# A two-layer graph network on one Trainium2 core: edge units dealt anew, logits made turned, and node sums in 64-node windows

## What is computed

```python
# layer 0, per edge e with source src and destination dst
msg = project_src(node)[src] + project_dst(node)[dst]       # 64 scalars + 32 vectors
m1  = tensor_product(msg, rsh(edge), rbf(edge) @ W_rbf)      # 96 scalars + 128 vectors
a   = leaky(m1_s @ W_alpha).reshape(e, 4, 16)                # leaky: a if a > 0 else 0.2 a
a   = sum(a * alpha_dot, -1)                                 # 4 logits per edge
alpha = softmax of a over the edges of one destination
val = gate(m1_s @ Ws_val, m1_v @ Wv_val); m2 = tensor_product(val, rsh)
agg = segment_sum(alpha * (m2 @ W_vlin), dst)                # then projected, added to x

# layer 1, per edge
w   = silu(rbf @ Wfc1) @ Wfc2
mid = w * tensor_product(f[src], rsh)                        # 384 numbers per edge
n   = segment_mean(mid, dst)                                 # then Wl2, Wa, Wsc per node
```

## Time and profile before

| | us |
|---|---|
| three timed runs | 8655.53, 8661.65, 8667.87 (median 8661.65) |
| profiled execution, span from first to last instruction | 8679.9 |
| PE busy | 7627.6 (88%) |
| DVE busy | 7274.4 (84%) |
| POOL busy | 6016.9 (69%) |
| ACT busy | 3252.4 (37%) |
| mean granted TensorE clock | 0.947 of full |

### The profile page before, as it was taken

How to read it: one execution, slowest core, us unless ns; L and a number is a source line. 1 busy time by engine, 2 the same in 40 slices (tenths; PEclk the granted TensorE clock), 3 DMA queues, 4 the chain that set the end, 5 groups by cost and what they waited for, 6 DMA issues and landing times. The chain is left out here.

```text
span 8679.9 us, 218293 instructions
## 1 busy us (share of the span) xinstructions
PE 7627.6 (88%) x60373; PEld 5771.5 (66%) x60374; DVE 7274.4 (84%) x17597; ACT 3252.4 (37%) x8375; POOL 6016.9 (69%) x5890
## 2 busy tenths in 40 slices
PE   2599999999999999999999999887968888888888
PEld 1487777877877787877787778776644444444445
DVE  4699999999999999999999999775368888888886
ACT  1244444444444444444444444332222222222223
POOL 0477777777777777777777777651037777777774
PEclk9799999999999999999999999987569999999999
DMA  4344444444444444444444444321012222222222
GB/s 53 78 101 99 102 100 101 102 100 101 101 102 101 101 101 99 102 100 100 100 101 102 101 102 100 77 75 29 11 37 67 67 67 67 67 67 67 67 67 61
DMA packets 616622, 725.52 MB, mean 84 GB/s; under 512 B 284132, under 2 KB 390884, under 8 KB 616573
## 3 DMA queue, kind: packets, MB, share of 16 engines
q0 software_dynamic: 225408, 385.00, 20.4%
q1 hardware_dynamic: 391165, 339.92, 15.3%
HBM read 708.40 MB, written 16.06 MB: 83 GB/s over the span
## 5 line engine op out<-in xcount | busy, mean ns | idle before, releaser
L778 PE MATMUL bank_pair<-w_msg,blocks 128*128 128x160 f32 (+2 forms) x15640 | 2078.7, 288 | 126.8 <-DVE blocks L1030 98.2
L720 POOL DMA_INDIRECT got_src<-src_tab,idx x1564 | 1661.5, 1062 | 659.4 <-POOL idx L714 358.5
L778 PEld LDWEIGHTS bank_pair<-w_msg,blocks 128*128 128x128 f32 x15640 | 1972.7, 192 | 218.5 <-DVE blocks L1030 218.5
L1504 POOL DMA_INDIRECT gotf<-f_tab,idx x1568 | 1702.3, 1086 | 514.2 <-issue 477.4
L720 POOL DMA_INDIRECT got_dst<-dst_tab,idx x1564 | 1486.3, 950 | 528.7 <-issue 503.7
L802 PEld LDWEIGHTS bank_pair<-weights_t,product 128*128 128x128 f32 x12896 | 1498.7, 195 | 309.9 <-issue 295.6
L802 PE MATMUL bank_pair<-weights_t,product 128*128 128x128 f32 x12896 | 1575.5, 281 | 9.5 <-ACT weights_t L932 8.2
L1545 PE MATMUL bank_pair<-val,to_node 128*128 128x385 f32 x3136 | 1247.6, 545 | 5.0 <-DVE val L1659 5.0
L1600 ACT ACTIVATE val<-pre,y_edge 128x160 f32<-128x160 f32 x1568 | 542.8, 417 | 1534.0 <-DVE pre L1640 1531.4
L1545 PEld LDWEIGHTS bank_pair<-val,to_node 128*128 128x128 f32 x3136 | 621.6, 208 | 536.8 <-issue 270.1
L767 PE MATMUL bank_pair<-edge,w_edge 64*128 64x512 f32 x3128 | 884.8, 642 | 9.5 <-DVE blocks L1030 9.5
(11 more groups left out here) (268 smaller groups left out, 11950.3 us busy)
## 6 DMA issues: line engine op xcount, KB each, us to landing
rbf<-in_rbf SPq DMA_DIRECT2D x391, 256.0 KB
dst_bc<-in_dst_rows SPq DMA_DIRECT2D x391, 256.0 KB
y<-in_y SPq DMA_DIRECT2D x391, 128.0 KB
y<-in_y SPq DMA_DIRECT2D x391, 96.0 KB
gotf<-f_tab,idx POOLq DMA_INDIRECT x1568, 2.7
got_src<-src_tab,idx POOLq DMA_INDIRECT x1564
got_dst<-dst_tab,idx POOLq DMA_INDIRECT x1564
rbf<-in_rbf SPq DMA_DIRECT2D x392, 32.0 KB, 1.7
```

The lines of the kernel that those rows point to most:

```text
L720: pool.indirect_dma_start(out=buf[slot][:, t, :], out_offset=None, in_=table[:, :], in_offset=bass.IndirectOffsetOnAxis(ap=idx[slot][:, c: ...
L778: return nc.tensor.matmul(to, blocks[rows, k, P * t:P * t + P], w_msg[rows, c0:c1], start=start, stop=stop)
L1504: pool.indirect_dma_start(out=got[k][:, t, :], out_offset=None, in_=f_tab[:, :], in_offset=bass.IndirectOffsetOnAxis(ap=idx[k][:, t:t + 1] ...
```

## The change

In layer 0 the sixteen pieces of the tensor product (32 channels by harmonic) are dealt anew over the four blocks, so that the scalars, the logit inputs and the vectors each need fewer columns: per tile four matmuls of 128, 128, 96 and 64 columns in place of five. The 64 logit inputs are no longer made beside the scalars but turned: `add_alpha` keeps `w_msg` in the array (64 columns) and streams the blocks (256 edges each into one half of the partitions). ACT makes `rl` from that, DVE one operation `leaky` (128 x 256), and `spread_logits` is a matmul with a constant `spread` that holds `alpha_dot`, each entry repeated 32 times; the multiplication, the reduction and `logits_wide` go. Both turned halves of `msg` now lie in different PSUM pairs. In ACT's list the weights come ahead of `th`, and `rl` last but for the copies of the turned message. SP loads 96 instead of 112 rows of `y8` per group.

```diff
-                def message_scalars(t):
-                    add_piece(scalar_tile(t), 0, slice(0, P), t, 0, True, False)
-                    return add_piece(scalar_tile(t), 2, slice(0, P), t, 3, False, True)
...
+                def add_alpha(k, piece, start, stop):
+                    first = MSG_FIRST[piece] + 128
+                    for half in range(2):
+                        last = nc.tensor.matmul(alpha[64 * half:64 * half + 64, :], w_msg[:, first:first + 64],
+                                                blocks[:, k, 256 * half:256 * half + 256], start=start, stop=stop)
+                    return last
+
+                def message_tile(t):
+                    add_piece(t, 0, LOW_S, MSG_C2, MSG_S + 96, True, False)
+                    add_piece(t, 3, HIGH_S, MSG_C2, MSG_S + 96, False, True)
+                    add_piece(t, 2, HIGH_V, MSG_C0, MSG_C1 + 32, True, False)
+                    return add_piece(t, 1, LOW_V, MSG_V, MSG_C1 + 32, False, True)
 
                 def spread_logits(slot):
-                    for t in range(TILES):
-                        last = nc.tensor.transpose(turn_low[:, P * t:P * t + P], logits_wide[slot][:, t, :], ident[:])
+                    for half in range(2):
+                        rows = slice(64 * half, 64 * half + 64)
+                        last = nc.tensor.matmul(spread_out[:, half, :], spread[rows, :], leaky[slot][rows, :], start=True, stop=True)
                     return last
...
                         for t in range(TILES):
-                            last = message_scalars(t)
-                        last.then_inc(s["message_s"], 1)
-                        for t in range(3):
-                            message_vectors(t)
+                            last = message_tile(t)
+                        last.then_inc(s["message"], 1)
+                        if mid:
+                            wait_apart(pe, s["top"], g, s["tick_p"])
+                        add_alpha(0, LOW_S, True, False)
+                        add_alpha(3, HIGH_S, False, True).then_inc(s["alpha"], 1)
                     if mid:
                         pe.wait_ge(s["weights"], g)
                         turn_weights().then_inc(s["weights_turned"], 1)
-                    if now:
-                        message_vectors(3).then_inc(s["message"], 1)
...
+                        if mid:
+                            act.wait_ge(s["leaky"], g)
+                        act.wait_ge(s["alpha"], g + 1)
+                        nc.scalar.activation(rl[:], alpha, ACT.Relu, scale=0.8).then_inc(s["relu"], 1)
...
-                        dve.tensor_tensor(lg[:], lg[:], adot[:].unsqueeze(1).broadcast_to([P, TILES, 64]), ALU.mult).then_inc(s["logit_step"], 1)
...
+                        dve.wait_ge(s["relu"], g + 1)
+                        dve.scalar_tensor_tensor(leaky[slot][:], alpha, 0.2, rl[:], ALU.mult, ALU.add).then_inc(s["leaky"], 1)
```

```diff
+                def add_tile(half, nodes, k, t, start, stop):
+                    for side in range(2):
+                        last = nc.tensor.matmul(win[half][WIN * side:WIN * side + WIN, :], nodes,
+                                                val[k][:, t, HALF1 * side:HALF1 * side + HALF1], start=start, stop=stop)
+                    return last
...
-                    dve.tensor_tensor(to_node[k % 2][:], iota_row[:].unsqueeze(1).broadcast_to([P, TILES, P]),
-                                      slot0[:, tile_dst(g, 1)].unsqueeze(2).broadcast_to([P, TILES, P]), ALU.is_equal)
+                    dve.tensor_tensor(to_node[k % 2][:], iota_row[:, 0:WIN].unsqueeze(1).broadcast_to([P, TILES, WIN]),
+                                      slot0[:, tile_dst(g, 1)].unsqueeze(2).broadcast_to([P, TILES, WIN]), ALU.is_equal)
...
-                    for j, n in enumerate(rows_of):
-                        last = nc.tensor.matmul(pQ[t % 2], turned[t % 2][0:n, j, :], w_last[0:n, j, :], start=j == 0, stop=j == 2)
+                    for k in range(4):
+                        cols = slice(WIN * (k // 2), WIN * (k // 2) + WIN)
+                        for part in range(2):
+                            last = nc.tensor.matmul(pQ[t % 2][WIN * part:WIN * part + WIN, :], turned[t % 2][:, 2 * part + k % 2, cols],
+                                                    w_last[:, k, :], start=k == 0, stop=k == 3)
```

330 lines of the change are left out of this document (176 added, 154 removed).

## The result

The changed kernel takes 8777.45 us (median of 4 runs, 8774.91 to 8791.91), the kernel before 8660.49 on the same chip (8655.53 to 8667.87). The ratio is 1.0135 by the medians, 1.014 with a 95% interval of 1.0125 to 1.0154 as measured: slower by about 117 us. The forecast was 8725 in a range of 8600 to 8850. The direction holds and so does the main mechanism; the size is 52 us short, and several steps behind it were wrong, as the experiments show. Some executions of any of these kernels run several per cent longer, whatever the kernel; medians and ratios here are those of the others.

A forecast was written before the change was run, and what follows sets the result against it. POOL was taken to bound both layers, with holding-up by DVE. Terms +36 - 15 (layer 0), +10 + 12 (layer 1), +22 (last stage) made +65 us: span 8679.9 to 8745, median 18 lower, about 8725; range 8600 to 8850.

The forecast's parts named there:

- POOL sets layer 0: Layer 0: POOL's list of 13.60 us per group plus its gathers' holding-up, 0.56, sets the time.
- the floor of PE that I set beside it: Layer 0: PE changes by -0.1 us per group to 13.3 to 13.4, just under POOL's 13.6.
- DVE now is the follower: PE waits for POOL's `edge` before it weighs: Layer 0: PE waits for POOL's `edge`, DVE for PE; DVE's phases are counted from the end of `edge`.
- The 0.10 that I added: Layer 0: in one cycle of ten a gather starts just inside L1053, losing 1.1 us; +36 us over 365 groups.
- +21 forecast: Layer 0 in all: +36 us for the steady groups and -15 for the last thirty.
- The tail: Layer 0's last 30 groups: 526 us, twelve extra windows at 8.7 us each; DVE's slack gives back 15 us.
- +44 forecast: Layer 1 and last stage: +10 us steady holding-up, +12 extra windows, +22 for 49 tiles at 1.6 us.
- the +12: Layer 1: five extra windows cost 12 us, 0 to 44 at the bounds, from 8.7 us per window.
- C: Rival, faster: idle DVE leaves gathers alone, the hold falls to 0.15 us in layer 0; 8578 us, chance 0.25.
- B: Rival, slower: layer 0's L1053 catches a gather every third cycle, costing 1.1 us; 8825 us, chance 0.15.
- D: Rival: column halves don't run together, PE bounds layer 0 at 14.6 us per group; 8942 us, chance 0.08.
- E: Rival: TensorE's clock falls in the emptier layer 1, costing 0.3 us per group; 8843 us, chance 0.07.

The follow-up runs named there:

- run 6: Changed kernel with one of the eight gathers per group left out in layer 0: 8713.60 us, ratio 1.0056 to the kernel before.
- runs 3, 4 and 6: 3 and 4: POOL's layer 0 list reordered, in the changed kernel (8785.28 us) and the kernel before (8742.2 us); 6: one gather left out (8713.60 us).
- run 1: Changed layer 0 with its weights' layout, in front of the old layer 1 and old last stage: 8723.72 us, ratio 1.0099 to the kernel before.
- run 2: Changed layer 1 and last stage behind the old layer 0: 8687.3 us, ratio 1.0052 to the kernel before.
- run 12: Old layer 0, changed layer 1 with `val` split in three, last stage transposing two tiles ahead: 10280.62 us, kernel before 9949.34 on that slower chip.
- run 8: Changed kernel without DVE's subtraction product<-product,across in layer 0: 8758.9 us, ratio 1.0121 to the kernel before.

## Why the prediction came out as it did

**POOL sets layer 0 (held, but it was half of the matter).** Its list of 13.60 us and 0.56 of holding-up make the 14.16 that was measured, and relieving PE or DVE gave 0.01 and 0.06 us. But the floor of PE that I set beside it, 13.3 to 13.4, was wrong. Three of its terms were right: the message -1.4 (measured -1.51), add_alpha +1.0 (+1.08), the wait for the copy of the weights +0.3 (+0.25). Missing were the spreading (+0.07) and the turning in two separate halves (+0.22). And I set out from PE's busy time, 13.49, as if that were its whole row: the 0.24 us of waiting ahead of the spreading stood in the trace of before. PE's floor is 13.97, 0.19 under the pace of the changed kernel, and run 6 stopped there, at 13.997.

**The sentence "DVE now is the follower: PE waits for POOL's `edge` before it weighs" failed.** No wait of PE for POOL stands in the profile after. DVE waits for PE a little (36.6 us in 2000), and its freed microsecond came back as 0.95 us inside `gated`, `sums` and `far`. The number that I derived from the phases, 0.56 of holding-up, is what was measured (0.56 between 2000 and 4000, 0.55 over the steady groups), yet the derivation can't claim it. The 0.10 that I added was to come from a gather that starts just inside the 1024-column product and loses 1.1 us. The share of gathers that start there and are held on by the products behind it went from 0.15 to 0.13 us; what grew, by 0.17, is the hold by the first product of 384 columns, L1085, which the derivation doesn't have. So the size of this term was luck. And runs 3, 4 and 6 show a POOL with more to spare held more.

**Layer 0 was mis-sized: +21 forecast, +86 by the timed ratio of run 1** (0.99%, interval 0.62 to 1.37), +44 between the two profiled executions including the start and the node stage. The steady part gave +28 for +36. The tail gave +7.5 for -15: twelve extra windows took nothing from DVE's slack. The start (+3.5) and the node stage (+5) were not in the sum. Of the gap of about 40 us between the two measurements, 18 are the profiled execution of the kernel before, which was that much slower than its timed runs. I carried that difference over to the changed kernel, whose profiled execution lies within 4 us of its timed ones. Taken from the span without it, the sum had been 8745. That makes about 62 us for layer 0; the rest up to 86 lies inside the interval of run 1 and has no cause shown.

**The tail was misread.** The window of 526 us in the earlier trace rows has 287 instructions of POOL, at 11 per group 26 groups and not 30, and DVE is not through with them at its end. The last thirty groups took 624.7 us by the starts of `gated`, so the twelve extra windows in them cost (624.7 - 30 x 14.08) / 12 = 16.9 us each, and not 8.7.

**Layer 1 and the last stage: +44 forecast, +45 measured in run 2 by the ratio, +50 by the medians.** The parts between the two profiled executions: steady groups -6 for +10, the last forty groups +15.3 for +12, last stage +33 for +22, and 8 us in front of it that I had not counted. So the sum came out by parts that missed in both directions, and the +12 rests on the misread price of 8.7 us. The passes do run in pairs, as the forecast had it; what was missing were the two gaps per tile, 0.40 us x 49 = 20.

**The rivals.** C (DVE out of the way of the gathers) and B (the 1024-column product catches a gather in every third group) did not come. D's condition is false: `add_alpha` costs 1.08 us for its eight passes, in pairs. The rule of the Trainium skill that was quoted for D ("TensorE: Matmul & The Clock Gate", "The mechanism": loads overlap only with another row group) is not borne out, as both halves used the same rows: in the last stage sixteen weight loads of 128 rows took 1.02 us beside sixteen passes that began with them at 8736.55. E's condition came, the clock of layer 1 fell to 0.75 (with PE busy for 0.75 of the stage, not 0.6), but its price did not: 5.545 us per group. On the slow chip of run 12 the clock was 0.67 and the group 7.25.

## What to carry to other kernels

Relieve engines in pairs before you name a bound: here one alone gave 0.01 or 0.17 us per group, both 0.54, because the second floor lay 0.19 under the first. Time that one engine is held inside its own operation by another engine's is both a cost and a hiding place for slack. A change of the holder's length can tell which: shorter operations on DVE gave 0.31 us per group in layer 1, less work on it 0.02 there and 0.06 in layer 0 (run 8). An edit that frees an engine which isn't the bound should be tried together with the edit that would use the room.

## What the runs showed of the hardware

- A gather held by DVE ends 0.82 us after the end of the operation that holds it: of the 285 gathers longer than 1.0 us between 7000 and 8000 in the changed kernel, every one ends 0.81 to 0.83 us after an operation of DVE. The one below ends at 7502.42, the `val` product at 7501.61. Cut into three, that product left the mean gather 56 ns above 947 instead of 136 (1003 and 1083).

```profile
7500.66 0.95 DVE L1694 TENSOR_TENSOR val<-pre,y_edge 128x768 f32<-128x768 f32 x1
7500.86 1.56 POOL L1542 DMA_INDIRECT gotf<-f_tab,idx  x1 [0.30 <-issue]
```

- Two column halves that use the same rows ran side by side with full 128-row weights too: sixteen loads and passes of 161 columns in about 1.1 us, where six single passes took 0.83.
- Four transposes of 128 x 128 and sixteen passes of 128 x 64 have 0.40 us of gaps between them at each change and back, with two buffers and with four, and half as much per tile when two tiles share a change. Where both were 128 x 128 there were none.
- The same code of layer 0 ran at 14.03 to 14.08 us per group in three profiled executions of the old one, and at 14.14 to 14.28 in three of the changed one, on different chips in part. In five of the six the difference is the holding-up of the gathers, 13.61 or 13.62 us without it (13.65 in the slowest). The cause of the different holding-up isn't shown.
